# A decoder layer on one core: batch 1's first projections in the ramp, GpSimd normalises, three places for rows

## The reference

```python
scores = jnp.einsum('bhqd,bhkd->bhqk', Q, K) / jnp.sqrt(jnp.float32(D_K))
attn = jax.nn.softmax(scores, axis=-1)
...
# WKV: per time step, with running maximum o
y = (A * p + E * vt) / (A * q + E)
...
h = jnp.square(jax.nn.relu(jnp.einsum('bsh,hi->bsi', residuals, up_w)))
y = jnp.einsum('bsi,ih->bsh', h, down_w) + moe_out
...
x = _layernorm(x + attention(x)); x = _layernorm(x + wkv(x, ctx)); x = layernorm3(x + ffn(x))
```

## Time and profile before

| | before |
|---|---|
| median of 3 runs | 216.61 us (215.62 to 217.32) |
| profiled execution | 216.79 us, its span 215.0 us |
| PE, PEld busy | 199.7, 111.7 us |
| DVE, ACT, POOL busy | 163.1, 150.9, 129.6 us |
| mean granted clock of TensorE | 0.991 |

### The profile page before, as it was taken

The page is one execution under the profiler, slowest core; times in us unless marked ns, Lnnn a source line. Parts: engine busy times, 40 slices in busy tenths (PEclk is TensorE's granted clock), DMA queues, the critical chain, the costliest instruction groups (busy, mean ns, idle before and its releaser), DMA issues.

```text
span 215.0 us, 4364 instructions
## 1 busy us (share of the span) xinstructions
PE 199.7 (93%) x1295; PEld 111.7 (52%) x1295; DVE 163.1 (76%) x392; ACT 150.9 (70%) x334; POOL 129.6 (60%) x256
## 2 busy tenths in 40 slices
PE   8889999979999899999999999999999998799970
PEld 3533543433433334575465445664655487698950
DVE  3469778778999899998979899976754837956274
ACT  2310477867899789989799879998967984763520
POOL 8995164753465724567476786867495493177622
PEclk9999999999999999999999999999999999999996
DMA  3145227943116602131000000010000000000001
GB/s 122 43 117 170 70 56 226 255 127 108 27 44 203 218 2 64 49 90 36 19 9 7 2 0 9 2 33 25 2 6 0 3 24 26 2 5 0 24 24 49
DMA packets 14759, 12.35 MB, mean 57 GB/s; under 512 B 3856, under 2 KB 12688, under 8 KB 14480
## 3 DMA queue, kind: packets, MB, share of 16 engines
q1 hardware_dynamic: 14064, 11.72, 19.0%
q10 hardware_dynamic: 672, 0.36, 0.6%
HBM read 6.57 MB, written 1.05 MB: 35 GB/s over the span
## 4 chain that ended last, share of the span: by engine, by line
PE 71%; DMA 8%; DVE 7%; ACT 6%; issue 5%; ACTq 1%; POOL 1%; POOLq 0%; DVEq 0%
PE ps_b L781 10%; PE ps_heads L629 10%; PE ps_exp L613 10%; PE ps_b L764 9%; DMA q_rows<-max_t 7%; PE ps_max L600 6%; PE ps_exp L635 4%; PE ps_exp L764 3%; PE ps_b L747 3%; PE ps_a L722 3%; PE ps_a L676 2%; ACT probs L812 2%; PE ps_a L665 2%; DVE maxima L1180 2%; PE ps_a L585 2%
## 5 line engine op out<-in xcount | busy, mean ns | idle before, releaser
L1180 DVE TENSOR_REDUCE maxima<-ps_max 128x2 f32<-128x512 f32 x128 | 85.0, 684 | 10.6 <-PE ps_max L600 9.7
L812 ACT ACTIVATE probs<-ps_exp 128x512 f32<-128x512 f32 x128 | 73.6, 599 | 14.6 <-PE ps_exp L613 14.1
L613 PE MATMUL ps_exp<-q_rows,k_rows 64*128 64x512 bf16 x128 | 46.2, 385 | 3.8 <-ACT probs L812 1.7
L600 PE MATMUL ps_max<-k_rows,q_rows 64*128 64x256 bf16 x256 | 47.4, 274 | 0.7 <-DMA q_rows<-q_parts 0.6
L613 PEld LDWEIGHTS ps_exp<-q_rows,k_rows 64*128 64x128 bf16 x128 | 11.4, 93 | 45.0 <-ACT probs L812 25.9
L629 PE MATMUL ps_heads<-probs,v_cols 128*32 128x512 f32 x256 | 33.9, 604 | 0.0
L781 PE MATMUL ps_b<-down_sb,inner_t 128*128 128x256 f32 x112 | 29.4, 388 | 0.7 <-ACT relu_t L943 0.7
L764 PE MATMUL ps_b<-x_t,up_sb 128*128 128x128 f32 x192 | 27.1, 285 | 1.1 <-DVE h L1367 1.1
L1061 POOL TENSOR_TENSOR rstd<-var_eps,minus_half 128x1 f32<-128x1 f32 x32 | 19.6, 611 | 11.7 <-DVE var_eps L1154 11.7
L764 PEld LDWEIGHTS ps_b<-x_t,up_sb 128*128 128x128 f32 x192 | 23.2, 191 | 6.0 <-issue 4.0
L781 PEld LDWEIGHTS ps_b<-down_sb,inner_t 128*128 128x128 f32 x112 | 19.4, 190 | 4.3 <-issue 1.5
(11 more groups left out here) (129 smaller groups left out, 345.2 us busy)
## 6 DMA issues: line engine op xcount, KB each, us to landing
q_rows<-q_parts SPq DMA_DIRECT2D x46, 64.0 KB, 2.1
x_t<-in_x_cols SPq DMA_DIRECT2D x4, 256.0 KB, 3.3
x_in<-in_x SPq DMA_DIRECT2D x4, 256.0 KB, 4.5
ctx_t<-in_ctx_cols SPq DMA_DIRECT2D x4, 256.0 KB, 3.0
up_sb<-in_up_w SPq DMA_DIRECT2D x1, 1024.0 KB, 6.1
down_sb<-in_down_w SPq DMA_DIRECT2D x1, 1024.0 KB, 6.1
out_y<-y_out SPq DMA_DIRECT2D x8, 128.0 KB, 1.7
post_sb<-in_w_post SPq DMA_DIRECT2D x1, 906.0 KB, 5.5
```

The costliest lines, as they stand in the source:

```text
L600: last = nc.tensor.matmul(ps_max[n % 2][:, r, :], q_rows[b][at:at + HALF, g, REP * jj + 2 * half + r, h * P:h * P + P], k_rows[b][at:at + ...
L613: nc.tensor.matmul(ps_exp[n % 2][:, :], k_rows[b][at:at + HALF, JH * g + jj, kt * P:kt * P + P], q_rows[b][at:at + HALF, g, REP * jj:REP * ...
L812: nc.scalar.activation(probs[n % 8][:, :], ps_exp[n % 2][:, :], ACT.Exp, scale=SCALE).then_inc(s_exp, 1)
L1180: nc.vector.tensor_reduce(maxima[s % 2][:, g, j // JH, 0, at:at + 2], ps_max[n % 2][:, :, :], AX, ALU.max, negate=True).then_inc(s_max, 1)
```

## The change

1. **Ramp.** x of batch 1 is loaded third, right behind the first two loads. TensorE runs batch 1's k projection between the two q projections of batch 0, and batch 1's q0 projection ahead of the first maxima unit. The 16 idle matmuls ahead of the first unit and the 15 behind units are gone; three groups of three (FILL) stand behind batch 1's k, batch 0's q1 and batch 0's v transposes.
2. **Who issues and does what in the ramp.** Of batch 0's k copies three go from ScalarE's to GpSimd's queue, and ScalarE issues three q copies instead of two. V's evacuation of batch 0 (vb) goes from VectorE to ScalarE; group 0's parts go from VectorE to GpSimd, its max_t evacuations from VectorE to ScalarE.
3. **GpSimd normalises.** For chunks 0 to 5, var_eps goes from VectorE to GpSimd in place of -mean, offset is dropped, and GpSimd does (x - mean) x rstd in one tensor_scalar instead of ScalarE's activation.
4. **Three places for rows** (ROT). Batch 3 uses batch 0's q_rows and k_rows again; its copies wait on SyncE for the 32nd exponential of all, and two more DMAs clear the maxima's rows. VectorE clears q_rows1 at the start, GpSimd only q_rows2.
5. **Twelve probs** buffers instead of eight (NPROBS).
6. **The table** AT is new nearly throughout, and LOAD_AFTER follows the load list.

```diff
-        "k": (1456, 2315, 2440, 3400),
+        "k": (1474, 1618, 2440, 3304),
...
-        "q0": (1503, 2379, 2792, 3624),
+        "q0": (1520, 1820, 2792, 3624),
...
+    FILL = 3
...
+    ROT = 3
+    NPROBS = 12
...
+            def rows_free(b):
+                sp.wait_ge(s_ones, ROT + (b >= 2))
+                if b == 1:
+                    sp.wait_ge(s_q1_zero, 1)
+                if b >= ROT:
+                    sp.wait_ge(s_exp, UNITS * TT * (b - ROT + 1))
+
             sp.dma_start(flat(x_t[0][:, :, :]), x_cols[0]).then_inc(s_xt[0], 16)
             sp.dma_start(qk_sb[:, KV_COLS:], w_qk[:, KV_COLS:]).then_inc(s_wq, 16)
+            sp.dma_start(flat(x_t[1][:, :, :]), x_cols[1]).then_inc(s_xt[1], 16)
...
+                                if b >= ROT and qp == 0:
+
+                                    sp.dma_start(row_block(q_rows[b % ROT][:, g], len(BLOCKS)),
+                                                 row_block(q_rows[1][:, g], len(BLOCKS) + 1)).then_inc(s_rows[b][g], 16)
...
-                    if n == 0:
-
-                        for done, value, n_idle in ((s_q2[0], 1, ROW_FILL), (s_q3[0], 1, 6 * ROW_FILL),
-                                                    (s_krows[0], 16 * len(BLOCKS), ROW_FILL)):
-                            pe.wait_ge(done, value)
-                            for k in range(n_idle):
-                                idle_matmul(ident_bf)
                     maxima_unit(n // UNITS, n % UNITS)
-                    if n < LAG:
-                        idle_matmul(ident_bf)
...
+                        if b == 1:
+                            for k in range(FILL):
+                                idle_matmul(ident_bf)
...
+            for kp, done in ((1, s_k2), (2, s_k3)):
+                gp.wait_ge(done, 1)
+                k_row_copies(gp, 0, kp, s_krows_pool)
+            gp.memset(q_rows[2][:], 0.0).then_inc(s_ones, 1)
...
+            def normalise(k, p, src, dst, done):
+                gp.wait_ge(s_rstd[k], p + 1)
+                for i in CHUNKS[p][1]:
+                    last = gp.tensor_scalar(dst[:, i, :], src[:, i, :], mean_var[k][:, i, 0:1], rstd[k][:, i:i + 1],
+                                            ALU.subtract, ALU.mult)
+                last.then_inc(done, 1)
...
-                                gp.tensor_scalar(neg_mean[k][:, ti], mean_var[k][:, ti, 0], -1.0, None,
-                                                 ALU.mult).then_inc(s_negmean[k], 1)
+                                gp.tensor_scalar(var_eps[k][:, ti], mean_var[k][:, ti, 1], EPS, None,
+                                                 ALU.add).then_inc(s_pool, 1)
```

More of the change, by code:

```diff
@@ L310, in decoder_layer @@
         rstd = [sb(f"rstd{i}", [P, TT]) for i in range(4)]
-        neg_mean = [sb(f"neg_mean{i}", [P, TT]) for i in range(4)]
-        offset = [sb(f"offset{i}", [P, TT]) for i in range(4)]
         ps_max = [ps(f"ps_max{i}", [P, 2, T]) for i in range(2)]
@@ L678, in _ @@
                             last.then_inc(s_q0 if b == 0 else s_a, 1)
+                            if b == 0 and g == 1:
+                                for k in range(FILL):
+                                    idle_matmul(ident_bf)
                     if AT["v"][b] == tick:
@@ L837, in _ @@
                                              bias=bkv_sb[0:KVD, 0:1]).then_inc(s_k1, 1)
+                    if b == 0 and AT["vb"][0] == tick:
+                        act.wait_ge(s_const, 1)
+                        a_filled(act, ("v", 0))
+                        nc.scalar.activation(
+                            heads_of(v_cols[0])[:, :, :, 0:HD],
+                            ps_a[:, 0:TT * KVD].rearrange("p (x j d) -> p x j d", j=GS, d=HD), ACT.Copy).then_inc(s_a_read, 1)
                     if b == 0 and AT["k2"][0] == tick:
@@ L968, in _ @@
             gp.memset(k_rows[0][:], 1.0).then_inc(s_ones, 1)
-            for i in range(2):
-                gp.memset(maxima[i][:, :, :, PARTS:HD], 0.0).then_inc(s_zeros, 1)
             own(gp.memset(ident[:], 0.0))
@@ L1205, in _ @@
                                                 ALU.add).then_inc(s_a_read, 1)
-                    if AT["vb"][b] == tick:
+                    if b >= 1 and AT["vb"][b] == tick:
                         dve.wait_ge(s_const, b + 1)
```

224 lines of the change are left out of this document (103 added, 121 removed), and 178 rows, old and new, of the table AT.

## The result

| | before | changed |
|---|---|---|
| median | 216.29 us (215.62 to 217.32, 4 runs) | 223.22 us (222.20 to 225.18, 4 runs) |
| ratio | | 1.033, 95% interval 1.024 to 1.041 |
| profiled execution, span | 216.79, 215.0 us | 222.85, 221.0 us |
| last matmul ends | 208.1 | 214.1 |

What follows compares the result with a forecast made beforehand. VectorE, with ScalarE close behind, was taken to bound the kernel before 85 us (VectorE pacing the ramp), TensorE behind; gains of 1.3 + 0.7 = 2.0 us take 216.79 to 214.8, 214.6 against the median; range 212.6 to 218.2.

Steps and rivals of the forecast that it cites:

- I take 0.5, as it has one tensor input: Normalising on GpSimd: each of 24 tensor_scalars of 128x256 would take 0.5 us, between a cast's 0.397 and a two-input operation's 0.730.
- the relief's 0.7: Before 85 us: normalising taken off ScalarE and VectorE, with twelve probs, would gain 0.7 us, bounds 0 and 2.3.
- Under a pace set by VectorE they cost nothing: Ramp: VectorE's reductions were taken to set the pace, so removing idle matmuls would give 0.
- The rival that I gave 0.16: Ramp: the clock falls to half speed, paid from the first exponents, losing 2.65 us, 217.3 in all; chance 0.16.
- each gap is only 0.4 us: Ramp: the argument against the clock falling, that TensorE's gaps between units are too short; by it 214.6.
- The ramp: First unit stays at 13.3 and the first exponents come earlier, a gain of 1.3 us, bounds 0 and 1.6.
- GpSimd's copies: Ramp: three k copies on GpSimd's queue, taken as no delay; at the upper end the start is 0.9 us later.
- The rows of the second set: Ramp: q copies issued after the second set's cast would land late, costing up to 0.4 us of the gain.
- 1.3 and 0: The ramp's gain, 1.3 us, and three places for rows, taken as 0 with an upper cost of 1.
- Behind 85 it is covered by TensorE: Behind 85 us: normalising moved to GpSimd would not count, since TensorE is busy throughout from 110 to 142.
- GpSimd's queue at 219.7: Rival: normalising ahead of the maxima's splitting in GpSimd's queue delays seven parcels, 5.1 us; chance 0.15.
- a stage 85 to 208 longer by 1 us: Sign of a wrong prediction: this stage, counted as TensorE's own work, changing by more than 1 us either way.

Runs made afterwards that it cites:

- e11: e2 with GpSimd's normalisation as a tensor_tensor of 0.61 us in place of 1.24, the mean's subtraction left out: 214.33 us, ratio 0.990.
- e10: Changed kernel with idle matmuls back, ScalarE normalising and the kernel before's order for the late stages: 214.86 us, ratio 0.993.
- e2: The changed kernel with one idle matmul put back behind each of the first 15 units of maxima: 221.85 us, ratio 1.021.
- e12: The kernel before with normalisation of batches 0 to 2 on GpSimd as a 0.61 us tensor_tensor, the mean's subtraction left out: 217.59 us, ratio 1.005.
- run 66: Not a label of a run: the words say that in e12 ScalarE has run 66 exponentials by 85 us, where the kernel before had 65.

## Why the prediction was wrong, point by point

**The failed term: "I take 0.5, as it has one tensor input".** The tensor_scalar took 1.24, 2.5 times that, and above the upper neighbour 0.730 that I had beside it. GpSimd got 20.4 us more in the profile (net of the row memsets that went), and this step, which I had booked at a gain of 0.7, lost 7 us (7.0 and 6.9 by the ratios). With the price near what I took (e11, 0.61) and the idle matmuls kept, the time is 214.3, 0.3 under the forecast. That closeness is partly luck: e10 gains 1.8 without any relief (0.993, interval 0.990 to 0.995, so 1.0 to 2.1 us), where I had 1.3, and no run shows the relief's 0.7.

**"Under a pace set by VectorE they cost nothing" (idle matmuls: 0).** The premise was a misreading of the earlier trace rows. In the ramp of before TensorE was busy for 11.48 of 11.50 us and waited for no reduction; a unit and its idle matmul took it 0.32 us each, which is the pitch of 0.64. So TensorE with its padding set the pace. And the clock fell at 17.4 and came back at 27.6. The rival that I gave 0.16 had the mechanism and the size: 2.65 us forecast, 2.4 and 2.5 measured. In the ramp half speed is hidden, as said, and it is paid from the exponents on (2.07 for a projection block). The Trainium skill (TensorE: Matmul & The Clock Gate, A second HAM failure mode: psum-queue depth-cycling) describes a clock that swings where matmul groups alternate with short idles between banks; the trace agrees in that the clock falls in such a stretch, with gaps of 0.21 us ahead of most units and of 0.79 and 0.82 ahead of two, but it falls once and stays down for 10.2 us. My argument against it, "each gap is only 0.4 us", was wrong. Without idle matmuls eight reductions stood 0.609 apart, where they had stood 0.642 apart:

```profile
12.59 4.87 DVE L1204 TENSOR_REDUCE maxima<-ps_max 128x2 f32<-128x512 f32 x8
```

Over fifteen units that is 0.5 us which the padding had cost and which my sum did not have.

**The ramp: right.** The first unit was at 12.14, in the other runs with this ramp at 12.1 to 13.2 (forecast 13.3). The spread is the start's: where the first projection took 1.87 to 1.91 us, as in before (1.89), the unit came at 13.1 to 13.2. From the first unit to the first exponents it is 9.96 us, 10.0 in e2 and 10.05 in e10, where before had 11.51: 1.5 us less, within my bounds of 0 and 1.6. There was no delay from GpSimd's copies, which took 0.60 each to issue and were all out at 9.26, the lower bound; VectorE had two instructions of 0.48 and 0.43 us beside them. The rows of the second set were late by 0.82 at 17.53 (up to 0.4 forecast). Together with three places and twelve probs it is worth 1.8 us (e10), where I had 1.3 and 0; by the interval the two are not told apart.

**"ScalarE and VectorE relieved before 85": not there.** In e12 the relief comes at a fair price in the old order, and the kernel is 0.9 us slower; ScalarE has run 66 exponentials by 85 us, before 65. e11's ratio (0.990 [0.986, 0.994]) is not told apart from e10's (0.993 [0.990, 0.995]), so the new order, even at the low price, has shown no gain over the old one.

**"Behind 85 it is covered by TensorE": the step that turned the sign.** TensorE was full because x always came in time. I asked what an engine's less work is worth there, not what more latency of x costs. My rival had GpSimd's queue at 219.7, but put the damage on the maxima's parts; the waits for maxima transfers fell from 1.6 us to 0.6, and the transposes of x waited instead. I had named a stage 85 to 208 longer by 1 us as a sign of being wrong; it came, for the last matmul is 6.0 later though the kernel was ahead at 85. The row of the maxima transfers now:

```profile
PE ps_exp L628 <- DMA q_rows<-max_t: 0.6, 2, 0.5
```

**The range.** Both rivals, the clock at +2.7 and GpSimd at +5.1, came true together, and I had summed chances as if only one could. By the ratios: 0.990 (e11) + 0.032 (price) + 0.011 (no idle matmuls) = 1.033, which is the ratio measured. The range left the GpSimd case out on the strength of a price that no row showed.

## What to carry to other kernels

Before work moves to another engine, measure that very form of instruction there: an instruction with the same shape but another opcode (cast 0.40, tensor_tensor 0.73) did not even bound the price from above. Where an engine stands full in the profile, ask of each result that it reads how late it may come; with 24 instructions 0.63 us longer the kernel lost 7 us. Idle matmuls in a stretch that would else have gaps bought the clock of the stage behind here; take them out only with a trace of the clock, and note that rivals on different engines add up.

An order written for one division of work does not carry another: GpSimd at 0.61 (without the mean's subtraction), VectorE at 0.51 (half of them) and ScalarE at 0.60 in the same places gave ratios of 0.990, 1.008 and 1.023. The version that beats both kernels is e10: the new ramp with its idle matmuls, three places and twelve probs, and the old order and ScalarE's normalisation behind it, 214.9 us, 0.7% under before.
